# First mixture of a fused two-layer kernel: order of the loads, start steps of the batches, and single products between half chunks

## The reference, cut to what matters

```
x = x + _L0_attn_ref(_layernorm(x), wq, wk, wv, wo)
    # Q, K, V = x wq^T, x wk^T, x wv^T (D = 64); energy = K^T V; out = (Q energy) sqrt(3/D) wo^T
h = _layernorm(x)
x = x + experts(h) + silu(h @ swg) * (h @ swu) @ swd      # 8 experts of 352, top 2; shared width 704
... layer 1: windowed attention, 8 experts of 1024, top 1
```

## Time and profile before

| | |
|---|---|
| median of 3 runs | 1455.87 us (1455.35 to 1459.08) |
| profiled execution | 1451.79 us, of which 1450.0 us are the span of the trace |
| PE busy | 1370.0 us, 94% of the span |
| DVE, ACT, POOL busy | 688.0, 469.6, 446.2 us |
| chain that ended last, by engine | PE 83%, DVE 6%, issue 4%, SP's queue 3%, ACT 2%, DMA 1%, POOL 1% |

### The profile page before, as it was taken

The page is one execution under the profiler, slowest core; times in us unless marked ns, Lnnn a source line. Parts: engine busy times, 40 slices in busy tenths (PEclk is TensorE's granted clock), DMA queues, the critical chain, the costliest instruction groups (busy, mean ns, idle before and its releaser), DMA issues.

```text
span 1450.0 us, 23596 instructions
## 1 busy us (share of the span) xinstructions
PE 1370.0 (94%) x7605; PEld 1014.2 (70%) x7605; DVE 688.0 (47%) x2480; ACT 469.6 (32%) x947; POOL 446.2 (31%) x533
## 2 busy tenths in 40 slices
PE   6578999999999999999999999999998999999998
PEld 4345656667777777656666666667665888999998
DVE  3543537433333333335888888878787122210000
ACT  2111211111211112121677666666655412111111
POOL 1110000044222222251454454544323433344442
PEclk9799999999999999999999999999999899999999
DMA  9700100012112122123655555545541578999996
GB/s 337 254 16 29 58 1 0 12 40 67 62 60 65 59 65 60 52 90 86 159 150 151 145 152 140 164 114 153 150 116 61 213 277 306 324 327 346 336 341 218
DMA packets 89463, 208.54 MB, mean 144 GB/s; under 512 B 11230, under 2 KB 45152, under 8 KB 79361
## 3 DMA queue, kind: packets, MB, share of 16 engines
q1 hardware_dynamic: 73664, 172.19, 36.3%
q0 software_dynamic: 12096, 32.13, 7.4%
q10 hardware_dynamic: 3584, 2.71, 0.6%
HBM read 155.74 MB, written 52.17 MB: 143 GB/s over the span
## 4 chain that ended last, share of the span: by engine, by line
PE 83%; DVE 6%; issue 4%; SPq 3%; ACT 2%; DMA 1%; POOL 1%; DVEq 0%; POOLq 0%; ACTq 0%
PE psum L781 12%; PE psum L948 10%; PE psum L958 9%; PE psum L658 9%; PE psum L760 6%; PE psum L854 5%; PE psum L807 5%; PE psum L669 5%; PE psum L829 4%; PE psum L878 3%; PE psum L908 2%; PE psum L887 2%; PE psum L739 2%; PE psum L769 2%; DVE work L1808 2%
## 5 line engine op out<-in xcount | busy, mean ns | idle before, releaser
L1808 DVE CUSTOM_DVE_ANT_0 work<-psum,mask 128x384 bf16<-128x384 f32 (+1 forms) x512 | 230.6, 485 | 73.9 <-PE psum L807 72.3
L781 PE MATMUL psum<-arena,work 128*128 x568 | 185.0, 469 | 0.5 <-issue 0.5
L807 PE MATMUL psum<-kz,qT 96*128 96x384 f32 (+1 forms) x512 | 171.5, 403 | 13.4 <-DVE small L1808 12.3
L1885 POOL DMA_INDIRECT work<-normed,token_of x71 | 67.3, 948 | 332.2 <-PE psum L739 211.4
L658 PE MATMUL psum<-arena 128*128 128x512 f32 x320 | 150.2, 613 | 0.0
L948 PEld LDWEIGHTS psum<-arena 128*128 128x128 f32 x1248 | 145.3, 192 | 2.2 <-issue 0.4
L948 PE MATMUL psum<-arena 128*128 128x128 f32 x1248 | 146.2, 275 | 0.0
L958 PE MATMUL psum<-arena 128*128 128x256 f32 x624 | 143.1, 383 | 0.5 <-issue 0.3
L1189 ACT ACTIVATE arena<-psum 128x384 f32<-128x384 f32 x256 | 112.2, 494 | 93.7 <-PE psum L829 92.8
L781 PEld LDWEIGHTS psum<-arena,work 128*128 128x128 f32 x568 | 102.1, 189 | 51.2 <-issue 2.0
L807 PEld LDWEIGHTS psum<-kz,qT 96*128 96x128 f32 x512 | 90.6, 195 | 66.2 <-DVE small L1808 40.2
(11 more groups left out here) (231 smaller groups left out, 2013.8 us busy)
## 6 DMA issues: line engine op xcount, KB each, us to landing
arena<-in_w SPq DMA_DIRECT2D x78, 1024.0 KB
strips<-hi SPq DMA_DIRECT2D x64, 256.0 KB
kz<-strips SPq DMA_DIRECT2D x64, 192.0 KB, 3.2
qT<-strips SPq DMA_DIRECT2D x32, 384.0 KB, 4.7
results<-work SPq DMA_DIRECT2D x71, 128.0 KB, 1.7
strips<-lo SPq DMA_DIRECT2D x32, 256.0 KB
normed<-work SPq DMA_DIRECT2D x14, 512.0 KB, 3.1
X<-in_x SPq DMA_DIRECT2D x8, 512.0 KB, 10.3
```

What stands on the lines that cost most here:

```text
L781: m = e.matmul(psum[:, pair[u], 0:INTER], xsT0[:, b % 2, c * P:(c + 1) * P], wu0[:, bass.ds(x, 1), c, u * INTER:(u + 1) * INTER], start=(c ...
L807: m = e.matmul(psum[:, bk, at:at + w], qT[0:ROWS_S, slot, half, i * P:(i + 1) * P], kz[slot][0:ROWS_S, hd, lo_key:hi_key], start=True, sto ...
L1808: e.tensor_tensor_reduce(masked[:, n % 2, 0:w], psum[:, bank_of["scores", u, i, hd], at:at + w], mask[:, P - off:P - off + w], 1.0, MASKED ...
```

## The change

The edits are all in the mixture stage. The amount of arithmetic and of data is the same.

- `BEGIN` of batches 2 to 7 is one step later (3, 5, ... 13). Their statistics of x stay at the step where they were (`begins`), so two steps lie between them and the products.
- PE's order inside a step: energy first; output product 0; first half of the chunk; fold; first k/v product; output products 1 and 2; second half of the chunk; second k/v product and q; output product 3. The short last chunk isn't cut.
- DVE's order: output 0; norm; statistics of the sum; statistics of the next x; outputs 1 and 2; the chunk's product; q's copy; output 3. ACT's order: energy; silu; fold; k and v.
- SP: the shared weights are issued after the first four batches of x, then the other four batches; SP waits until the xT of batches 4 to 7 have landed and only then issues the experts' weights.
- `ROUTED_AT` follows `BEGIN` and becomes 21.

```diff
-BEGIN, LEAD, LAST_STAGE = (0, 1, 2, 4, 6, 8, 10, 12), 8, 7
+BEGIN, LEAD, LAST_STAGE = (0, 1, 3, 5, 7, 9, 11, 13), 8, 7
...
+def begins(step):
+
+    return [b for b in range(B) if BEGIN[b] - (b > 1) == step]
...
                 for b in due(s, 7):
                     pe_turn_batch(e, 1, b, ring)
+                for b in due(s, 2):
+                    pe_energy(e, b, ring)
                 for b in due(s, 4):
-                    pe_out0(e, b, (0, 1), ring)
+                    pe_out0(e, b, 0, ring)
+                pairs = [(b, c, next_of(H_RING)) for b, c in chunk(s, 0)]
+                for b, c, pair in pairs:
+                    pe_shared_up(e, b, c, pair, range(1) if c < NC - 1 else range(2))
                 for b in due(s, 3):
                     pe_fold(e, b, ring)
-                for b in due(s, 2):
-                    pe_energy(e, b, ring)
                 for b in due(s, 1):
-                    pe_qkv0(e, b, ring)
-                for b, c in chunk(s, 0):
-                    pe_shared_up(e, b, c, H_RING)
+                    pe_kv0(e, b, 0, ring)
                 for b in due(s, 4):
-                    pe_out0(e, b, (2, 3), ring)
+                    pe_out0(e, b, 1, ring)
+                    pe_out0(e, b, 2, ring)
+                for b, c, pair in pairs:
+                    if c < NC - 1:
+                        pe_shared_up(e, b, c, pair, range(1, 2))
+                for b in due(s, 1):
+                    pe_kv0(e, b, 1, ring)
+                    pe_q0(e, b, ring)
+                for b in due(s, 4):
+                    pe_out0(e, b, 3, ring)
...
         def sp_mix(e):
-            for b in range(B):
+            for b in range(4):
                 e.dma_start(X[:, b * TPB:(b + 1) * TPB, 0:E], x_in[:, b, :, :]).then_inc(x_loaded[b], 16)
                 e.dma_start(xnT_all[:, b, :, :], a["xT"][:, b, :, :]).then_inc(xT_loaded[b], 16)
...
+            for b in range(4, B):
+                e.dma_start(X[:, b * TPB:(b + 1) * TPB, 0:E], x_in[:, b, :, :]).then_inc(x_loaded[b], 16)
+                e.dma_start(xnT_all[:, b, :, :], a["xT"][:, b, :, :]).then_inc(xT_loaded[b], 16)
+            for b in range(4, B):
+                e.wait_ge(xT_loaded[b], 16)
             for i, n in enumerate(("wg", "wu")):
```

More of the change, by code:

```diff
@@ L176, in norm_numbers @@
     for step in range(MIX_STEPS):
-        for k, norm in ((5, 1), (0, 0)):
-            for b in due(step, k):
+        for norm, batches in ((1, due(step, 5)), (0, begins(step))):
+            for b in batches:
                 number[norm, b] = len(number)
@@ L589, in pe_centre, with pe_kv0, pe_q0 @@
             m.then_inc(bank_full[bk], 1)
-        def pe_qkv0(e, b, ring):
+        def pe_kv0(e, b, h, ring):
             e.wait_ge(xT_loaded[b], 16)
[L593 to L601, removed]
+            bk = next_of(ring)
+            fill(e, ("kv", b, h), bk)
+            for u in range(2):
+                t = 2 * h + u
+                for c in range(EC):
+                    m = e.matmul(psum[:, bk, u * KVG:(u + 1) * KVG], xnT_all[:, b, c, t * P:(t + 1) * P],
+                                 w_c[:, c, 0:KVG], start=(c == 0), stop=(c == EC - 1))
+            m.then_inc(bank_full[bk], 1)
+        def pe_q0(e, b, ring):
             bk = next_of(ring)
@@ L624, in pe_fold, with pe_out0, pe_shared_up @@
             e.matmul(psum[:, bk, 0:XW], en_sb[0:D0, b % 2, :, :].rearrange("p r d -> p (r d)"), w_o, start=True, stop=True).then_inc(bank_full[bk], 1)
-        def pe_out0(e, b, tiles, ring):
-            if tiles[0] == 0:
+        def pe_out0(e, b, t, ring):
+            if t == 0:
                 e.wait_ge(ew_made, b + 1)
                 e.wait_ge(q_made, b + 1)
[L630 to L636, removed]
+            bk = next_of(ring)
+            fill(e, ("out", b, t), bk)
+            e.matmul(psum[:, bk, 0:XW], qT_sb[:, b % 4, t * P:(t + 1) * P], ew_sb[:, b % 2, :],
+                     start=True, stop=True).then_inc(bank_full[bk], 1)
+        def pe_shared_up(e, b, c, pair, halves=range(2)):
             w = SC[c]
-            pair = next_of(ring)
             if c == 0 and halves[0] == 0:
@@ L1070, in act_mix @@
                                  .broadcast_to([D0, 2, D0]), ACT.Copy).then_inc(en_made, 1)
+                for b, c in chunk(s, 0):
+                    act_silu(e, b, c)
+                for b in due(s, 3):
+                    if b >= 2:
+                        e.wait_ge(*done["out", b - 2, TPB - 1])
+                    e.wait_ge(*done["fold", b])
+                    e.activation(ew_sb[:, b % 2, :], psum[:, bank_of["fold", b], 0:XW], ACT.Copy,
+                                 scale=scale).then_inc(ew_made, 1)
                 for b in due(s, 1):
                     act_kv(e, b)
-                for b, c in chunk(s, 0):
-                    act_silu(e, b, c)
                 if s == ROUTED_AT:
@@ L1306, in dve_mix @@
                     dve_gate(e, b)
+                for b in due(s, 5):
+                    e.wait_ge(a_added, TPB * (b + 1))
+                    for t in range(TPB):
+                        dve_stats(e, b * TPB + t)
+                    dve_scale(e, 1, b)
+                for b in begins(s):
+                    e.wait_ge(x_loaded[b], 16)
+                    for t in range(TPB):
+                        dve_stats(e, b * TPB + t)
+                    dve_scale(e, 0, b)
                 for b in due(s, 4):
-                    dve_out0(e, b, (0, 1))
+                    dve_out0(e, b, 1)
+                    dve_out0(e, b, 2)
+                for b, c in chunk(s, 0):
+                    dve_hidden(e, b, c)
                 for b in due(s, 1):
```

41 lines of the change are left out of this document (12 added, 29 removed).

## The result

| | before | after |
|---|---|---|
| median | 1455.68 us (1455.35 to 1459.08, 4 runs) | 1434.2 us (1431.07 to 1445.1, 4 runs) |
| ratio, 95% interval | | 0.9875 (0.9846 to 0.9904) |
| profiled execution | 1451.79 us | 1431.44 us, span 1429.7 us |
| mean granted clock of it | 0.978 | 0.986 |
| PE busy | 1370.0 us | 1360.3 us, 95% |

The change is faster, by 1.25% as the ratio has it (the two medians lie 21.5 us apart). The profiled executions differ by 20.3 us of span; the prediction's sum was 19.3.

A forecast was written before the change was run, and what follows sets the result against it. PE bounds the kernel, busy for 94% of the span, so savings before 155 us move everything behind. 8.4 - 4.0 + 12.6 + 3.3 - 1.0 = 19.3 us off 1455.87 gives 1436.6 us; range 1428.5 to 1446.

The forecast's parts named there:

- (1): Steady steps up to 155 us: PE's waits go, gaining 12.6 us, plus 3.3 us of low clock behind them.
- (2): Output products issued singly on PE: costs 1.0 us, 0.7 for changing products and 0.3 at the short last chunk.
- (3): PE's hole behind batch 0's write: stays but moves to output 3 of batch 3, with 8.4 us of work done inside it.
- (4): SP's wait before the experts' weights: delays batch 0's write and PE, costing 4.0 us, bounds 1.7 and 4.4.
- (5): Load order: earlier shared weights gain nothing by themselves, and later x of batches 4 to 7 costs nothing.
- (6): Routing one step later: 5 to 6 us stay to spare before the fetched rows are used, so it costs nothing.
- A: PE's steady waits come back in the new place, at output 3; gain only 9 us, 1447 us; chance 0.13.
- B: PE's hole is gone or much shorter; up to 7 us more, 27 in all, 1429 us; chance 0.07.
- C: DVE's row in even steps outlasts PE's 9.8 us; slower than before, 24 us, 1460 us; chance 0.04.
- D: No difference: experts' weights come so late that the hole takes all back; chance 0.04 with the like.

The follow-up runs named there:

- e6: Changed kernel with both sets of DVE's statistics moved back to the end of their step; 1428.3 us (1 run).
- e10: Changed kernel with PE's energy product moved behind output 1, DVE's order as changed; 1433.8 us (1 run).
- e9: Changed kernel with the start steps of the kernel before, and with them routing at step 20; 1438.3 us (1 run).
- e11: Changed kernel with three orders undone: statistics last, norm ahead of output 0's addition, energy behind output 1; 1436.7 us (1 run).
- e13: Kernel before with one edit: PE's energy product ahead of outputs 0 and 1; 1428.7 us (1 run).
- e12: Kernel before with one edit: DVE's statistics of the sum ahead of q's copy and the chunk's product; 1434.7 us (1 run).
- e4: Changed kernel with the write of batch 0's normed rows issued ahead of the experts' weights; 1425.7 us, ratio 0.9813.
- e5: Changed kernel with only SP's wait for the xT of batches 4 to 7 removed; 1428.3 us, ratio 0.9825.
- e1: Changed kernel with SP's load order as before and no wait on xT; 1428.5 us, ratio 0.9816.
- e3: Changed kernel with routing one step earlier again, at step 20; 1437.4 us, ratio 0.9895.
- e8: Changed kernel with batch 0's write ahead of the experts' weights, SP's xT wait removed and routing at step 20; 1422.5 us, ratio 0.9783.
- e7: Changed kernel with each chunk in one piece at the place of its first half; 1440.8 us (1 run).

## Why the prediction was right, point by point

- **(1) The steady steps, 12.6 and 3.3 us.** Right in size: PE is busy for 84.86 of 85.00 us. The reason was too narrow. The prediction's walk has energy first and takes rstd from the step before, because the statistics have moved. e6 puts the statistics back and the waits stay away, e10 and e9 do so for energy and for the start steps, and of the kernels tried only the one with three orders back at once (e11) brings them back. On the kernel before, energy alone takes them away (e13), and the statistics alone all but 1.2 us (e12).
- **(2) Single products, 1.0 us.** The 0.7 us in it were nothing. The four outputs of batch 7 and the chunk among them took 5.25 us in the kernel before (chain of waits, 0.89 + 3.43 + 0.93, from 146.63 to 151.88) and 5.21 after (0.45 + 1.72 + 0.89 + 1.72 + 0.45, from 130.48 to 135.69), so taking them apart cost nothing. The 0.3 us came in: output 3 behind the short last chunk, which waits for DVE as forecast (chain of waits of after, 102.92 to 103.49, 0.57 us, once):

```profile
102.46 0.46 PE psum L638 x2
...
102.95 0.50 DVE X L1361
...
103.49 0.71 PE psum L638 x2
```

- **(3) The hole.** Place, cause and waiting instruction as forecast. PE stopped near 57.5 us (66.83 - 9.37), 0.5 us ahead of the forecast 58 to 61, DVE stood at the norm at 53.8 (forecast 53 to 57), and the hole was 9.37 us of 6 to 10. PE took up work at 66.83 us, for 67.6. All 8.4 us of work were done ahead of it. e4 shows the cause. The working of PE's arrival was off, though: its own terms add up to 61.1, and it took 37.7 us of busy time from a stretch in which the kernel before ran partly at the lower level (0.77 in the earlier trace rows from 39.12 to 53.65 us). After had full clock up to the hole and was busy for 41.7 us, where 46.1 were forecast. It changed nothing at the end: had PE come later, the hole would only have been shorter.
- **(4) SP's wait, 4.0 us.** The landing at 35.9 us was right (35.96). The delay of the write was 64.76 - 61.57 = 3.2 us and of PE 3.19, inside the bounds of 1.7 and 4.4, and e5 and e1 give back 2.7 and 3.1 of it. I leaned too far to the upper bound. The 2.0 us that the prediction quotes from the Trainium skill ("DMA: Bandwidth & Descriptors", "Anatomy of one DMA") are given there for DMAs issued by GpSimd, while SP issues these; the sum doesn't use them.
- **(5) Earlier shared loads.** Nothing gained that shows, as forecast: e1, without them, takes up work after the hole at 63.70 us, and e5, with them, at 64.17. The 1.6 us between their first rows are the clock behind the wait for the shared sum. Later x cost nothing either.
- **(6) Routing one step later.** This is the step that failed, by 3.9 us. It looked at the fetch alone: the token list was ready in time, and the rows were used 9.1 us after the fetch was issued at 268.16, so that cover held. It didn't follow DVE's own queue. With one step's shift the four routing pieces of a step fall on the step ahead of batch 3's shared sum, the addition comes late, and PE waits 2.31 us and, in this execution, loses 1.6 to the clock (of the eight profiles with this wait four have the low clock behind it, so the second part isn't fixed). e3 takes the wait away.
- **Rivals.** A (waits at L620 or L638 every two steps) did not come, and e11 shows waits of up to 2.0 us a time with three orders back. B (no hole) came only where the write was moved (e4, e8). C would have shown as waits that grow from step to step; there are none. D would have wanted the write 23 us later; it was 3.2.

The forecast of 1436.6 us against 1434.2 is thus closer than its terms deserve, and that part is luck: 3.9 us of loss are missing in (6), and against them stand 0.7 + 0.8 taken off too much in (2) and (4) and the 3.1 us by which the untouched stages of the profiled execution were shorter.

## What to carry to other kernels

When an edit shifts the start step of background work (here the routing), list what it newly stands ahead of on its own engine, not only whether its result is still in time. A write that frees a buffer belongs ahead of bulk loads that nobody needs soon: 512 KB landed 3.4 us after issue in front of them and 10.9 us behind them. Before re-timing a stage, try to move only the product that is held up by somebody else's wait: one such move (e13) reached the same place as the whole change, whose further gains of about 7 us went into its two losses. So it also pays to test each part of a change alone.

## What the runs showed of the hardware

**The clock in a stage that no edit touches.** The attention of the second layer took 530.9 us in the profile of after, 541.6 in that of e1 and 541.7 in that of e7; the mean granted clock of the whole profiles is 0.986, 0.977 and 0.979. Busy time by stretch of after, and then of e1, over the same 100 us and, for e1, over the whole stretch:

```profile
803.30:903.30 100.00, 95.21 (x657) 67.97 (x658) 81.95 (x349) 65.03 (x130) 46.64 (x63) 1.00 0.48 137
```

```profile
800.00:900.00 100.00, 95.39 (x619) 68.30 (x623) 78.10 (x331) 60.85 (x121) 43.96 (x60) 0.93 0.46 132
575.50:1117.10 541.60, 509.08 (x3102) 354.49 (x3099) 394.95 (x1601) 298.15 (x590) 224.70 (x295) 0.96 0.44 125
```

PE is equally busy but does fewer instructions, at a granted clock of 0.93. What lowers the clock there is open.

**Idle time and the clock.** The holes of 10 and 9.4 us were followed by a granted clock of 0.60 (before, 63.64 to 70.60 us) and 0.62 (after, 66.83 to 73.79) over the next 7 us, that is mostly by the lower level of 1.2 GHz. For shorter waits the length alone doesn't decide. The wait of 3.7 to 3.8 us of the transposition (L565) that ends near 43 us was followed by full clock in after, e3 and e5, and by the lower level in e1, e4 and e8 (0.50 from 44 to 48 us in each). In the kernel before, 2.43 us of waiting ahead of a transposition (L560), ending at 41.55, were followed by it too (0.50 from 42 to 48 us). The wait of 2.3 us for the shared sum was followed by the lower level in after, e1, e4 and e10 (3.52 to 3.60 us for the down product) and by full clock in e5, e6, e7 and e11 (1.97 us). Timeline of e7:

```profile
219.54 1.97 PE L673 MATMUL psum<-arena,work 128*128 128x256 f32 x8 [2.32 <-DVE X L1381]
```

The 3.3 us that the prediction gave to the clock behind the steady waits came in, but such a term is a matter of chance per wait, and I can't say from these rows what decides.
